# Compact state update and four-head Gram products in a gated-delta-rule kernel

## The reference

```python
x = x + 0.5 * ffn(layernorm(x))
x = x + attn(layernorm(x))
x = x + 0.5 * ffn(layernorm(x))
```

```python
k = rmsnorm(x by heads) * k_norm_w;  q = k;  v = -(x @ W.T)
def step(S, (q_t, k_t, v_t)):
    S = S * lam
    err = v_t - k_t @ S
    S = S + beta * outer(k_t, err)
    return S, q_t @ S
out = layernorm(static_out + o) * o_norm_w + o_norm_b
```

## Time and profile before

| What | us |
|---|---|
| median of three runs | 1498.38 |
| lowest and highest of them | 1492.49, 1502.06 |
| profiled execution, its own time | 1506.1 |
| its span | 1504.3 |
| TensorE busy (matmuls) | 1375.4 |
| VectorE busy | 889.1 |
| ScalarE busy | 602.5 |
| GpSimd busy | 274.0 |

### The profile page before, as it was taken

How to read it: one execution, slowest core, us unless ns; L and a number is a source line. 1 busy time by engine, 2 the same in 40 slices (tenths; PEclk the granted TensorE clock), 3 DMA queues, 4 the chain that set the end, 5 groups by cost and what they waited for, 6 DMA issues and landing times.

```text
span 1504.3 us, 61982 instructions
## 1 busy us (share of the span) xinstructions
PE 1375.4 (91%) x27811; PEld 1264.2 (84%) x27811; DVE 889.1 (59%) x2208; ACT 602.5 (40%) x1465; POOL 274.0 (18%) x350
## 2 busy tenths in 40 slices
PE   4899999999999999989988989899899999999797
PEld 4889888989989888788877878888889889898786
DVE  2657786868678467468548744943445455454522
ACT  2243433433334334334432533344344545544332
POOL 0022121111211111113303310320311304040500
PEclk9999999999999989899889998999999999999999
DMA  4011111122121332242224233224324243332000
GB/s 133 1 57 57 60 58 64 56 101 75 68 78 67 98 94 79 85 162 71 77 68 139 78 101 123 78 84 133 108 65 149 71 143 84 112 103 94 1 29 29
DMA packets 64201, 125.39 MB, mean 83 GB/s; under 512 B 12352, under 2 KB 33088, under 8 KB 61888
## 3 DMA queue, kind: packets, MB, share of 16 engines
q1 hardware_dynamic: 63936, 121.43, 25.2%
HBM read 62.13 MB, written 59.24 MB: 81 GB/s over the span
## 4 chain that ended last, share of the span: by engine, by line
PE 71%; DVE 16%; issue 5%; ACT 5%; DVEq 0%; ACTq 0%
PE ps L440 35%; PE ps L507 8%; PE ps L1052 7%; PE ps L852 6%; PE ps L1036 4%; PE ps L699 3%; PE ps L671 3%; DVE ln_bn L83 2%; ACT gates L457 2%; PE ps L400 2%; DVE prod L774 2%; DVE inv L777 1%; ACT ffn_rows L107 1%; PE ps L492 1%; PE ps L680 1%
## 5 line engine op out<-in xcount | busy, mean ns | idle before, releaser
L440 PE MATMUL ps<-cst,wt 128*128 128x128 f32 x2688 | 355.6, 285 | 9.2 <-DVE cst L485 8.8
L440 PEld LDWEIGHTS ps<-cst,wt 128*128 128x128 f32 x2688 | 322.5, 195 | 21.1 <-DVE cst L485 10.4
L440 PE MATMUL ps<-ffn_rows,wt 128*128 128x128 f32 x2304 | 305.7, 285 | 15.9 <-ACT gates L457 4.9
L440 PEld LDWEIGHTS ps<-ffn_rows,wt 128*128 128x128 f32 x2304 | 282.3, 197 | 25.1 <-issue 13.6
L479 DVE TENSOR_TENSOR fc<-gates,cst 128x256 f32<-128x256 f32 x112 | 55.2, 493 | 292.5 <-ACT gates L457 292.3
L457 ACT ACTIVATE gates<-ps,colv 128x128 f32<-128x128 f32 x448 | 127.3, 366 | 222.5 <-PE ps L440 222.5
L1052 PE MATMUL ps<-e,kgb 32*128 32x64 f32 x4032 | 127.6, 273 | 3.0 <-issue 2.6
L1052 PEld LDWEIGHTS ps<-e,kgb 32*128 32x128 f32 x4032 | 118.7, 186 | 11.3 <-issue 4.6
L852 PE MATMUL ps<-inv_cols,kv 32*32 32x32 f32 x8192 | 102.2, 198 | 24.8 <-issue 14.5
L1141 POOL TENSOR_TENSOR ffn_rows<-ffn_rows,rowv 128x256 f32<-128x256 f32 x64 | 52.7, 860 | 396.0 <-DMA ffn_rows<-x_scratch 396.0
L852 PEld LDWEIGHTS ps<-inv_cols,kv 32*32 32x32 f32 x8192 | 87.0, 109 | 44.2 <-issue 26.7
(11 more groups left out here) (118 smaller groups left out, 1759.1 us busy)
## 6 DMA issues: line engine op xcount, KB each, us to landing
kg_scratch<-kg_rows SPq DMA_DIRECT2D x32, 512.0 KB, 3.9
xs_scratch<-xs_out SPq DMA_DIRECT2D x32, 512.0 KB, 3.6
xsb<-xs_scratch SPq DMA_DIRECT2D x64, 256.0 KB, 3.4
kgb<-kg_scratch SPq DMA_DIRECT2D x256, 64.0 KB, 2.6
ffn_rows<-x SPq DMA_DIRECT2D x32, 256.0 KB, 3.5
x_scratch<-ffn_rows SPq DMA_DIRECT2D x32, 256.0 KB, 2.8
e_scratch<-e SPq DMA_DIRECT2D x256, 32.0 KB, 1.7
ffn_rows<-e_scratch SPq DMA_DIRECT2D x8, 1024.0 KB, 6.1
```

What stands on the lines that cost most here:

```text
L440: mm = pe.matmul(banks[g][:, col:col + P], wt[:, w, k, m * P:(m + 1) * P], rhs, start=(x in (0, FI)), stop=(k == KT - 1 and (t == 0 or x > ...
```

## The change

It does the following. The gap of zeros goes out of the decayed keys: `kg_rows`, `kg_scratch` and `kgb` have 16 columns per lane. An update matmul has 32 rows, 64 columns and 64 moving columns, and writes 64 partitions: row groups 0 and 1 to partitions 0 to 63, 2 and 3 to 64 to 127. All 32 lie in banks 4 and 5, and the fences hold for these alone (S_PIECES). `zbd` has for k below 16 the states in rows 0 to 63 and the units in rows 64 to 127, and the other way round above; `xsb` and `xs_rows` are laid out to match, and a hop's `xsb` is loaded by four DMAs. The states are now copied by VectorE in one masked product of 64 x 1024 and by ScalarE in four scaled copies of 32 x 256. There are four masked copies of the keys, one per head of four: two by VectorE, two by ScalarE. A Gram matmul has 64 rows, 32 columns and 4 x 32 moving columns; each of `g0` to `g3` has 32 of them, in the same two banks. In the set-up, the memsets of `kgb` and `kg_rows` go and three small tables come. The two h buffers have a tensor of their own.

```diff
+S_PIECES = (4, 5)
...
-        if bank >= 4:
+        if bank in S_PIECES:
             behind_hop[key] = last_hop
...
-        kgb = sb("kgb", [P, 2, SETS * 8 * 2 * HD])
+        kgb = sb("kgb", [P, 2, SETS * 8 * HD])
...
-        kg_rows = sb("kg_rows", [P, 2 * BD])
+        kg_rows = sb("kg_rows", [P, BD])
+        hs_more = sb("hs_more", [P, 4 * D])
...
-        key_half = sb("key_half", [P, BD])
+        key_half = sb("key_half", [P, 2 * BD])
...
-                pe.wait_ge(z_done, SETS * min(BEHIND_HOP[key] + 1, HOPS - 1))
+                pe.wait_ge(z_done, STATE_OPS * min(BEHIND_HOP[key] + 1, HOPS - 1))
...
-                for e in range(2):
+                for e in (0, 1):
                     dve.tensor_scalar(keyTm[:, e, :, :], keyT[:, 8 * gh:8 * gh + 8, :], w_mask[:, e:e + 1], None, ALU.mult).then_inc(halves, 1)
...
-            gh, pp = f // 2, f % 2
+            gh = f // 2
             if "a" in parts:
-                pe.wait_ge(halves, 4 * n + 2 * gh + 2)
+                pe.wait_ge(halves, 8 * n + 4 * gh + 4)
...
-            for g in [2 * "abcd".index(part) + e for part in parts for e in range(2)]:
+            for gi in ["abcd".index(part) for part in parts]:
+                g = 4 * f + gi
                 for q in range(Q):
                     for par in range(2):
-                        row = slice(32 * (2 * pp + par), 32 * (2 * pp + par) + 32)
+                        row = slice(64 * par, 64 * par + 64)
                         tok = slice(32 * q, 32 * q + 32)
-                        mm[par] = pe.matmul(dst[par].ps[tok, 64 * g:64 * g + 64].rearrange("p (e i) -> p e i", e=2),
-                                            keyT[row, 8 * gh + g, tok], keyTm[row, :, g, tok],
+                        mm[par] = pe.matmul(dst[par].ps[tok, P * gi:P * gi + P].rearrange("p (e i) -> p e i", e=SETS),
+                                            keyT[row, g, tok], keyTm[row, :, g % 8, tok],
                                             start=True, stop=True, skip_group_check=True)
...
+            elif name in ("km0", "km1"):
+                gh = int(name[2])
+                emptied(act, "kt", n, 2 * gh)
+                emptied(act, "kt", n, 2 * gh + 1)
...
+                for e in (2, 3):
+                    act.activation(keyTm[:, e, :, :], keyT[:, 8 * gh:8 * gh + 8, :], ACT.Copy, scale=w_mask[:, e:e + 1]).then_inc(halves, 1)
...
-        S_BANKS = psum[:, 4 * 512:8 * 512].rearrange("p (k w) -> p k w", w=SETS * HD)
+        S_BANKS = psum[:, 4 * 512:6 * 512].rearrange("p (k w) -> p k w", w=SETS * HD)
+        STATE_OPS = 1 + SETS
...
-            sp.dma_start(xsb[:, 2 * C * LS * a:2 * C * LS * a + C * LS], xs_d[j][:, C * LS * a:C * LS * (a + 1)]).then_inc(xs_in[a], 16)
+            for h in range(2):
+                at = h * 3 * C * C + 2 * C * C * a
+                for v in range(2):
+                    rows = 64 * (h ^ v)
+                    sp.dma_start(xsb[rows:rows + 64, at:at + C * C],
+                                 xs_d[j].rearrange("(c v p) f -> v c p f", c=SETS, v=2)[v][:, :, 2 * C * C * h + C * C * a:2 * C * C * h + C * C * (a + 1)]).then_inc(xs_in[a], 16)
...
-            for k in range(4, 8):
+            for k in S_PIECES:
                 wait_pos(pe, bank[k].read, AHEAD_OF_HOP[s][k])
...
                     k = 8 * g + kk
-                    mm = pe.matmul(S_BANKS[:, k, :], kgb[32 * g:32 * g + 32, a, P * kk:P * kk + P], es[a][32 * g:32 * g + 32, 64 * kk:64 * kk + 64],
+                    out_rows = slice(64 * (g // 2), 64 * (g // 2) + 64)
+                    mm = pe.matmul(S_BANKS[out_rows, k % C, :], kgb[32 * g:32 * g + 32, a, 64 * kk:64 * kk + 64], es[a][32 * g:32 * g + 32, 64 * kk:64 * kk + 64],
                                    start=True, stop=True, skip_group_check=True)
...
-            for c in by_act(s):
-                act.copy(state_of(zbd, c), state_of(S_BANKS, c)).then_inc(z_done, 1)
+            for c in range(SETS):
+                rows, cols = slice(64 + 32 * (c // 2), 96 + 32 * (c // 2)), slice(HD * c, HD * c + HD)
+                act.activation(zbd[rows, C:2 * C, cols], S_BANKS[rows, :, cols], ACT.Copy,
+                               scale=mask4[rows, c:c + 1]).then_inc(z_done, 1)
...
+            dve.tensor_tensor(zbd[0:64, 0:C, :].rearrange("p k (c d) -> p k c d", c=SETS),
+                              S_BANKS[0:64, :, :].rearrange("p k (c d) -> p k c d", c=SETS),
+                              mask4[0:64, :].unsqueeze(1).unsqueeze(3).to_broadcast([64, C, SETS, HD]),
+                              ALU.mult).then_inc(z_done, 1)
...
-                link(dve.memset(kgb, 0.0))
...
-                link(dve.memset(kg_rows, 0.0))
...
```

More of the change, by code:

```diff
@@ L993, in build @@
         late = kg_rows
-        fg = Ffn("f2", "fr2", "ct2", hs + [late[:, BD + k * 512:BD + (k + 1) * 512].rearrange("p (e d) -> p e d", e=2) for k in range(2)],
+        fg = Ffn("f2", "fr2", "ct2", hs + [hs_more[:, k * 512:(k + 1) * 512].rearrange("p (e d) -> p e d", e=2) for k in range(2)],
                  0, stats_buf[2], [cols_of(io[:, BD:2 * BD]), cols_of(late[:, 0:BD])])
@@ L1375, in tables_dve @@
                 link.wait()
[L1376 removed]
+                link(dve.tensor_scalar(w_mask, mask4, w_key[:, 1:2], None, ALU.mult))
                 link.wait()
[L1378 removed]
+                link(dve.scalar_tensor_tensor(out=w_x, in0=mask[:, 0:1], scalar=w_key[:, 1:2], in1=mask[:, 1:2], op0=ALU.mult, op1=ALU.add))
                 link(dve.memset(zbd, 0.0))
[L1380 removed]
                 link.wait()
[L1382 to L1384 removed]
+                link(dve.tensor_copy(zbd[64:128, 0:C, :], ident[64:128, 64:128].unsqueeze(1).to_broadcast([64, C, 64])))
+                link(dve.tensor_copy(zbd[0:64, C:2 * C, :], ident[0:64, 0:64].unsqueeze(1).to_broadcast([64, C, 64])))
                 for a in range(2):
[L1386 removed]
+                    link(dve.tensor_copy(kgb[:, a, :].rearrange("p (l w) -> p l w", w=HD),
                                          unit[1 - a].unsqueeze(1).to_broadcast([P, LS, HD])))
@@ L1393, in tables_dve @@
                 link(dve.tensor_copy(g_tok, src.ps[:, P:P + H]))
-                for c in range(SETS):
-                    row = slice(32 * c, 32 * c + 32)
-                    link(dve.tensor_copy(lam_z[row, :], src.ps[row, 2 * P:3 * P].rearrange("p (k c) -> p c k", c=SETS)[:, c, :]))
-                link.wait()
-                link(dve.tensor_tensor(xsb[:, C * LS:2 * C * LS].rearrange("p (j k) -> p j k", k=LS),
-                                       unit[0].unsqueeze(2).to_broadcast([P, HD, LS]),
-                                       lam_z.unsqueeze(1).to_broadcast([P, HD, LS]), ALU.mult))
-                link(dve.memset(kg_rows, 0.0))
+                lane_lam = src.ps[:, 2 * P:3 * P].rearrange("p (k c) -> p c k", c=SETS)
+                link(dve.tensor_scalar(lam_z, lane_lam[:, 0, :], mask4[:, 0:1], None, ALU.mult))
+                for c in range(1, SETS):
+                    link.wait()
+                    link(dve.scalar_tensor_tensor(out=lam_z, in0=lane_lam[:, c, :], scalar=mask4[:, c:c + 1], in1=lam_z,
+                                                  op0=ALU.mult, op1=ALU.add))
+                link.wait()
+                for h in range(2):
+                    link(dve.tensor_scalar(lam_z[:, C * h:C * h + C], lam_z[:, C * h:C * h + C], half_of[:, h:h + 1], None, ALU.mult))
+                link.wait()
+                for h in range(2):
+                    link(dve.tensor_tensor(xsb[:, h * 3 * C * C + C * C:h * 3 * C * C + 2 * C * C].rearrange("p (j k) -> p j k", k=C),
+                                           unit16.unsqueeze(2).to_broadcast([P, HD, C]),
+                                           lam_z[:, C * h:C * h + C].unsqueeze(1).to_broadcast([P, HD, C]), ALU.mult))
                 link.wait()
```

63 lines of the change are left out of this document (30 added, 33 removed).

## The result

The changed kernel takes 1438.25 us (median of four runs, 1435.31 to 1440.92) against 1496.74 us of the kernel before (four runs, 1492.49 to 1502.06). The ratio is 0.9598, with a 95% interval of 0.9565 to 0.9631, so 58.5 us less. 1436.9 was predicted. The profiled execution took 1437.1 us (span 1435.3).

What follows compares the result with a forecast made beforehand. TensorE, busy 91% of the span, was taken to bound the kernel. Terms of -41.5, -13, -5, -4, +4 and -2 sum to -61.5 us, from 1498.4 to 1436.9 us; range 1405 to 1480.

Steps and rivals of the forecast that it cites:

- The price of an update: State update on TensorE: bound by weight loads, so halved loads take it from 1.95 to 1.12 us, 0.83 less.
- The number of updates that count: State update: 50 of 63 updates shorten the span, from 98 us on the chain; 50 x 0.83 = -41.5 us.
- a microsecond off TensorE in such a step is a microsecond off the span: Plain 8.82 us step: TensorE never stops, so its savings pass fully to the span if ScalarE and VectorE keep up.
- The Gram part: Gram products on TensorE: half the records, a part falls from 0.78 to 0.53 us; -13 us.
- a term of 4 us for the supply of instructions: TensorE's instruction supply: 1024 matmuls fewer reduce waits for "issue"; -4 us (+10 to -20).
- The fences: Banks 6 and 7: refills no longer wait for state copies, nor the update for their readers; -5 us (0 to -8).
- The state copies: VectorE's copies 0.17 us shorter, ScalarE's 0.7 longer; nothing lost in plain steps, +4 us overall (0 to +15).
- The rival in which they take the update's gain: ScalarE's four copy pieces cost well over 0.47 us each, state c comes last, update's gain goes: 1473 us; 14%.
- The masked copies: ScalarE's two more key copies per half, about 1.0 us each, fit in its idle time: 0.
- Transfers: DMA and SyncE: xs in four issues adds about 1.2 us per hop, but loads run two hops ahead: 0.
- Set-up: Start of kernel: memsets of kg_rows and kgb go, some small products come; -2 us (0 to -5).
- two-bank rivals: Update's row groups collide at one bank: only two work at a time, 1493 us (11%), or drain in turn, about 1780 (7%).

Runs made afterwards that it cites:

- e8: Kernel before, update matmuls loading only 64 of 128 weight columns, four banks kept: update 1.09 us, whole 24 us below that kernel's median in one run.
- e12: Kernel before, update matmuls multiplying only 32 of 64 moving columns, full weight load of 128 columns: update 1.91 us against 1.95.
- e5: Changed kernel, GpSimd's adds of the bias to x1 wait until VectorE's LayerNorm chain is through: ratio 0.9565 to the kernel before.
- e3: Changed kernel, xs loaded by one DMA per hop instead of four, its products stored in four pieces: 1512.79 us.
- e6: Changed kernel, ScalarE's first half of the LayerNorm applications (L107) moved behind gates, state copies and tanh: 1404.05 us.
- e11: Changed kernel, L107 behind the gates from block 9 on, and GpSimd's x1 adds waiting for the LayerNorm chain in blocks 7 and 8: 1393.35 us.
- e1: Changed kernel with its Gram part undone (64 Gram matmuls of 32 rows and 64 moving columns per group), compact state kept: 1471.73 us.
- e9: Changed kernel, every Gram matmul split into two of 64 moving columns, still 64 rows, four key copies kept: 1477.13 us.
- e2: Changed kernel with the fences of before, so refills of banks 6 and 7 wait for the state copies again: 1457.74 us.
- e4: Changed kernel, ScalarE's two masked copies of the keys made for the first block alone: 1445.74 us.
- e7: Changed kernel with both GpSimd's x1 adds waiting for the LayerNorm chain and L107 moved behind the gates: 1408.26 us.
- e10: Changed kernel, L107 moved behind the gates only in the steps of blocks 9 and later: 1396.64 us.

## Why the prediction came out right, and where it was wrong

The number held within 2 us, and that is luck: several terms were off by more than that, in both directions. The terms, point by point:

- **The price of an update** was right: 0.83 us less predicted, 0.86 measured, for the reason given (e8, e12). The plain step is 0.82 us shorter.
- **The number of updates that count** was wrong. The term took 50 x 0.83 from the share of the chain and read it off plain steps. The update alone is worth about 24 us, not 41.5 (e8). The step that failed is "a microsecond off TensorE in such a step is a microsecond off the span": it held for the plain steps, and not for steps 4 and 7, in which ScalarE holds the gates behind a LayerNorm chain. Such a chain by itself could only have kept these steps as long as they were. They became longer, by 15.9 us for eight of them, and three things are seen to do it: GpSimd's additions now cover more of the chain in steps 4 of blocks 11 to 13 (e5), which took 3.5, 2.4 and 3.0 us before and takes 4.9, 4.4 and 6.2, ScalarE's longer state copies push tanh and gates back in steps 7 (e8 against the changed kernel), and the clock falls behind the longer halts. Why the additions fall there now is open: a later load of x1 explains a small part at most (e3). With the gates first, the same hops take 267.4 us and less (e6 to e11).
- **The Gram part** was 13 us by its records, and these did fall by 13.8, though a part takes 0.60 us start to start and not 0.53. It is worth 33 (e1). The prediction had a term of 4 us for the supply of instructions, and did not price its sequel: waits for "issue" fell from 33.4 to 16.5 us, and the time at the lower clock fell too. e9 puts the gain on the number of records. That it runs through these halts is argued: e9 and e1 have as many of them, but 42 and 68 us at the lower clock.
- **The fences** were 5 us by a wait of 5.8, and are worth 20 (e2): the wait was priced at its length alone, while in e2 the idle time doesn't grow and all of the 20 us lie in busy time at the lower clock.
- **The state copies**, +4: TensorE's waits for them rose from 7.5 to 11.4 us. The direct price was right. The rival in which they take the update's gain didn't come in plain steps. In steps 7 it came in part: the gates start 0.5 us and the tanh 0.9 us later than in e8, which has the old copies. The larger part is the order of L107 and L462 on ScalarE, which no rival named.
- **The masked copies** at 0 held as far as e4 can tell, with 1.14 us each in place of 1.0.
- **Transfers** at 0 stand as far as e3 can tell. **Set-up**, -2: the first phase is 10.3 us shorter; it holds (9159 - 7879) / 32 = 40 Gram parts, which by the timeline (0.60 us a part against 0.78) make 7. The first phase of the kernel before also ran in e8 and e12, and that of the changed kernel in e2, e5, e6, e7, e10 and e11. The means are 518.9 us of three and 511.1 of seven (506.7 to 515.9), 7.8 apart, so at most 1 us is left for the set-up.

What was missing altogether is TensorE's clock. In hops 0 to 33 the kernel before spent 81.5 us at 1.2 GHz, the changed one 23.8. Work at half speed takes twice the time, so 57.7 us fewer are worth at most 29 us. The traces give less. Busy time in this stage fell by 53.9 us; 34 updates at 0.86 are 29 of it and 24 of the 64 Gram parts 5, which leaves about 20, or 0.34 us for each us at the lower clock. In e2 it is 20.7 for 51.5, or 0.40. And over the 32 executions of the kernel before that stand beside the experiments, with granted clocks of 0.953 to 0.971, the span grows by 0.32 us for each us more at the lower clock, with scatter. Over whole executions the time at the lower clock is 113 us before (mean of 32), 79 in the changed kernel (of 4), 117 in e1 and 122 in e2 (of 6 each), so the pattern doesn't rest on the profiled executions alone.

In the prediction's sum the clock stands nowhere. The too large update term hid it: -41.5 was too much by 17, and Gram, supply and fences too little by 31. These don't cancel to the measured sum, since the pieces don't add up: update 24 (e8), fences 20 (e2) and Gram part 33 (e1) make 77 of 58.5 us. The update and the fences together, with the new copies, give 27 (e1). Parts that remove time at the lower clock, or lengthen the same steps 4 and 7, can't be priced one by one.

What the order of ScalarE costs in the last hops is 35 us in the changed kernel (301.2 - 266.1, e10). How much of it was there before wasn't measured, but an estimate can be made from the traces: 300.7 us before, less 25 for the updates, less 6.5 of idle time (13.0 against e11's 6.5), less 3.4 for 6.7 us at the lower clock, leaves 266, and e11 takes 266.6. So about 10 of the 35 us were there before, and the 25 of the updates all come once the gates go first.

For the two-bank rivals, the Trainium skill's rule ("TensorEngine Tiling (Array Packing)", Gotcha 1), that different row tiles can't access one PSUM bank simultaneously, had 11% and 7%. The measurement decides: not so here, for outputs in different partitions of a bank.

## What to carry to other kernels

Look for the operation that a shorter critical engine will expose: in every kind of step, not only in the plainest one, find the chain with which another engine holds back the critical one, see what else could fall on that chain when the steps move, and order that engine by who waits for its result. Count a halt of TensorE at more than its length wherever the granted clock stands below 1 behind it; here a microsecond at the lower clock cost 0.3 to 0.4 us. If many small matmuls run in a row, fewer and larger ones can give more than the busy time of their records.
